# Norm stage: the shared down product in one tile shape and two banks, the low part in two instructions; table stage: constants in another order

## Time and profile before

| | us |
|---|---|
| median of the timed runs (3) | 3653.11 (3651.51 to 3653.34) |
| the profiled execution, time | 3649.46 |
| its span | 3647.7 |
| norm stage, from to | 0 to 414 |
| table stage | 414 to 453 |
| attention with the experts | 453 to about 3433 |
| output | to the end |
| granted PE clock, mean | 0.984 of full |

### The profile page before, as it was taken

How to read it: one execution, slowest core, us unless ns; L and a number is a source line. 1 busy time by engine, 2 the same in 40 slices (tenths; PEclk the granted TensorE clock), 3 DMA queues, 4 the chain that set the end, 5 groups by cost and what they waited for, 6 DMA issues and landing times. The chain is left out here.

```text
span 3647.7 us, 59807 instructions
## 1 busy us (share of the span) xinstructions
PE 3527.4 (97%) x16231; PEld 2094.8 (57%) x16232; DVE 2534.3 (69%) x3254; ACT 1686.6 (46%) x3126; POOL 2711.4 (74%) x2322
## 2 busy tenths in 40 slices
PE   7999569999999999999999999999999999999899
PEld 5777445555555555555555555555555555555487
DVE  7888657777777777777777777777777777777444
ACT  4444324444444444444444444444444444444443
POOL 1111138888888888888888888888888888889611
PEclk9999779999999999999999999999999999999899
DMA  7766455666666666666666666666666666664386
GB/s 217 218 200 208 155 125 125 160 171 171 171 171 171 171 171 171 171 171 171 171 171 171 171 171 171 171 171 171 171 171 171 171 171 171 171 171 125 118 313 228
DMA packets 393627, 635.53 MB, mean 174 GB/s; under 512 B 48048, under 2 KB 214640, under 8 KB 393584
## 3 DMA queue, kind: packets, MB, share of 16 engines
q1 hardware_dynamic: 370800, 603.54, 59.4%
q0 software_dynamic: 14336, 23.08, 3.0%
q10 hardware_dynamic: 8448, 8.39, 0.6%
HBM read 306.91 MB, written 126.12 MB: 119 GB/s over the span
## 5 line engine op out<-in xcount | busy, mean ns | idle before, releaser
L1089 DVE TENSOR_REDUCE merged<-psum 128x1 f32<-128x1024 f32 x1024 | 1206.2, 1220 | 731.0 <-PE psum L917 729.2
L1052 ACT ACTIVATE probs<-psum 128x512 f32<-128x512 f32 x2048 | 1083.6, 600 | 1159.5 <-PE psum L891 744.4
L1216 POOL TENSOR_TENSOR sums<-sums,probs 128x512 f32<-128x512 f32 x768 | 981.0, 1277 | 94.9 <-ACT probs L1052 40.2
L1217 POOL TENSOR_TENSOR sums<-sums,probs 128x512 f32<-128x512 f32 x768 | 982.4, 1279 | 0.0
L932 PE MATMUL psum<-probs,v_sb 128*64 128x512 f32 x4096 | 930.2, 596 | 0.0
L888 PE MATMUL psum<-q_full,k_full 128*128 128x512 f32 x2048 | 877.3, 428 | 0.0
L891 PE MATMUL psum<-q_rest,k_rest 65*128 65x512 f32 x2048 | 812.5, 397 | 0.0
L932 PEld LDWEIGHTS psum<-probs,v_sb 128*64 128x64 f32 x4096 | 283.7, 137 | 559.2 <-issue 496.1
L888 PEld LDWEIGHTS psum<-q_full,k_full 128*128 128x128 f32 x2048 | 388.5, 190 | 196.6 <-issue 95.3
L1117 DVE RECIPROCAL sum_all<-sum_all 128x128 f32<-128x128 f32 x512 | 448.8, 918 | 28.3 <-ACT sum_all L1060 28.3
L964 PE MATMUL psum<-x_t,w_qk 128*128 128x512 f32 x1536 | 411.9, 404 | 38.0 <-DVE w_d L1082 27.5
(11 more groups left out here) (143 smaller groups left out, 3085.2 us busy)
## 6 DMA issues: line engine op xcount, KB each, us to landing
x_t<-xt SPq DMA_DIRECT2D x118, 1024.0 KB
k_full<-high SPq DMA_DIRECT2D x256, 256.0 KB
v<-values SPq DMA_DIRECT2D x64, 512.0 KB, 3.2
w_qk<-wqk_parts SPq DMA_DIRECT2D x64, 512.0 KB, 4.0
q_full<-high SPq DMA_DIRECT2D x128, 256.0 KB
q_full<-low SPq DMA_DIRECT2D x128, 256.0 KB
k_rest<-low SPq DMA_DIRECT2D x128, 256.0 KB
q_rest<-high SPq DMA_DIRECT2D x128, 256.0 KB
```

Of the source, the lines that this page charges most:

```text
L1052: nc.scalar.activation(probs[:, kt, h, :], ring[ring_place(g, j) % RING], ACT.Exp, scale=SCALE).then_inc(probs_ready, 1)
L1089: nc.vector.tensor_reduce(out=merged[:, col:col + 1], in_=work[:, 2 * h:2 * h + 2, :].rearrange("p b c -> p (b c)"), axis=AX, op=ALU.max, ...
L1216: nc.gpsimd.tensor_tensor(sums[:, half, 0, :], first[:, 0, :], probs[:, kt, 0, :], ALU.add)
L1217: nc.gpsimd.tensor_tensor(sums[:, half, 1, :], first[:, 1, :], probs[:, kt, 1, :], ALU.add).then_inc(sums_added, 1)
```

## The change

- The second tiles of the down product's operands, `ws_d1` and `hidden1`, get 128 partitions; partitions 64 to 127 are set to zero once, by DVE at the start, and PE waits for that (`rest_zero`) in the first unit. All down matmuls then use 128 rows.
- The second round of the down product goes to bank 4 (`up_ps`) and doesn't wait for a copy. In the next unit, the c = 1 products wait for the first copy, the up products for the second.
- POOL's low part is two instructions of 512 columns.
- Table stage: the triangle `upto` is finished first, then the iotas, `carry` last. PE's counting matmuls wait for `ones` alone, its rows for `upto`.

```
-    ws_d1 = sb("ws_d1", [F2, D])
+    ws_d1 = sb("ws_d1", [P, D])
...
-    hidden1 = sb("hidden1", [F2, HALF])
+    hidden1 = sb("hidden1", [P, HALF])
...
-        sp.dma_start(ws_d1[:], io["ws_d"][P:F, :]).then_inc(weights_in, DMA)
+        sp.dma_start(ws_d1[0:F2, :], io["ws_d"][P:F, :]).then_inc(weights_in, DMA)
...
-            nc.gpsimd.tensor_tensor(xt_low[:, par], xt32[:, par], f32(xt_high[:, par]), ALU.subtract
-                                    ).then_inc(xt_lows, 1)
+            for k in range(KD):
+                last = nc.gpsimd.tensor_tensor(xt_low[:, par, k, :], xt32[:, par, k, :], f32(xt_high[:, par, k, :]),
+                                               ALU.subtract)
+            last.then_inc(xt_lows, 1)
...
                 act.wait_ge(down_filled, 2 * u + n + 1)
+                bank = up_ps if n else down_ps
                 nc.scalar.copy(shared[:, par, 2 * n:2 * n + 2, :],
-                               down_ps.rearrange("p (t d) -> p t d", d=D)).then_inc(shared_ready, 1)
+                               bank.rearrange("p (t d) -> p t d", d=D)).then_inc(shared_ready, 1)
...
+        nc.vector.memset(hidden1[F2:P, :], 0.0).then_inc(rest_zero, 1)
+        nc.vector.memset(ws_d1[F2:P, :], 0.0).then_inc(rest_zero, 1)
         norm(0, 0, linked(0, [0]))
...
-                pe.wait_ge(*((shared_ready, 2 * u) if c else (hidden_ready, 2 * (u - 1) + 1)))
+                pe.wait_ge(*((shared_ready, 2 * u - 1) if c else (hidden_ready, 2 * (u - 1) + 1)))
             for out, col in ((down_ps, 2 * P),) if c else ((gate_ps, 0), (up_ps, P)):
+                if out is up_ps and not known(u, 1):
+                    pe.wait_ge(shared_ready, 2 * u)
...
             pe.wait_ge(hidden_ready, 2 * u + 2)
+            if known(u, 1):
+                pe.wait_ge(rest_zero, 2)
             for n in range(2):
-                if n or not (isinstance(u, int) and u == 0):
-                    pe.wait_ge(shared_ready, 2 * u + n)
+                bank = up_ps if n else down_ps
                 for t in range(2):
                     cols = slice((2 * n + t) * P, (2 * n + t + 1) * P)
-                    nc.tensor.matmul(down_ps[:, t * D:(t + 1) * D], hidden0[:, cols], ws_d0[:],
+                    nc.tensor.matmul(bank[:, t * D:(t + 1) * D], hidden0[:, cols], ws_d0[:],
                                      start=True, stop=False)
-                    last = nc.tensor.matmul(down_ps[:, t * D:(t + 1) * D], hidden1[:, cols], ws_d1[:],
+                    last = nc.tensor.matmul(bank[:, t * D:(t + 1) * D], hidden1[:, cols], ws_d1[:],
                                             start=False, stop=True)
...
         nc.gpsimd.memset(ones[:], 1.0).then_inc(consts, 1)
         nc.gpsimd.memset(upto[:], 1.0).then_inc(consts, 1)
-        nc.gpsimd.memset(carry[:], 1.0).then_inc(consts, 1)
+        pool.wait_ge(consts, 2)
+        nc.gpsimd.affine_select(out=upto[:], in_=upto[:], compare_op=ALU.is_ge, fill=0.0, base=0,
+                                pattern=[[1, P]], channel_multiplier=-1).then_inc(consts, 1)
...
-        pool.wait_ge(consts, 6)
-        nc.gpsimd.affine_select(out=upto[:], in_=upto[:], compare_op=ALU.is_ge, fill=0.0, base=0,
-                                pattern=[[1, P]], channel_multiplier=-1).then_inc(consts, 1)
+        nc.gpsimd.memset(carry[:], 1.0).then_inc(consts, 1)
+        pool.wait_ge(consts, 7)
         nc.gpsimd.memset(carry[:, :, 0:1], 0.0).then_inc(consts, 1)
...
-        pe.wait_ge(consts, 8)
+        pe.wait_ge(consts, 1)
         flat = masks[:].rearrange("p j e -> p (j e)")
...
+        pe.wait_ge(consts, 3)
         for n in range(8):
             pe.wait_ge(counts_out, n + 1)
```

More of the change, by code:

```diff
@@ L157, in norm_stage @@
     pads_stored = sem("pads_stored")
+    rest_zero = sem("rest_zero")
     x_v = io["x"].rearrange("(u t p) d -> u p t d", p=P, t=UNIT)
@@ L457, in unit @@
                     dve.wait_ge(down_filled, 2 * u)
-                nc.vector.tensor_tensor(hidden[:], up_rest[:] if c else up_ps, silu[0:rows, c, :], ALU.mult
+                nc.vector.tensor_tensor(hidden[0:rows, :], up_rest[:] if c else up_ps, silu[0:rows, c, :], ALU.mult
                                         ).then_inc(hidden_ready, 1)
             assert count[0] == VEC or not more, count[0]
+        nc.vector.memset(hidden1[F2:P, :], 0.0).then_inc(rest_zero, 1)
+        nc.vector.memset(ws_d1[F2:P, :], 0.0).then_inc(rest_zero, 1)
         norm(0, 0, linked(0, [0]))
```

## The result

| | before | after |
|---|---|---|
| median of the timed runs | 3653.23 (4 runs, 3651.51 to 3653.65) | 3610.26 (4 runs, 3606.79 to 3610.97) |
| the profiled execution, time | 3649.46 | 3610.97 |
| its span | 3647.7 | 3609.2 |
| attention's first matmul starts | 454.45 | 408.39 |
| from there to the end of the span | 3193.25 | 3200.81 |

The ratio is 0.9881, with a 95% interval of 0.9864 to 0.9898: 43 us faster. The forecast was 3610.

What follows compares the result with a forecast made beforehand. PE was taken to bound the norm stage, with DVE close behind. Gains 8.8 + 26.6 + 1.0 + 2.0 + 4.4 = 42.8, say 43 us, off the median 3653.11 gave 3610 us, range 3600 to 3626.

Steps and rivals of the forecast that it cites:

- first three units (third S): Start of the norm stage: third unit's S at 89.5 instead of 98.30, gain 8.8 us (bounds 7.8 and 10.2).
- S: Start of the first down product of a unit in the norm stage, the mark for periods.
- twelve periods: Norm stage, third to fifteenth unit's S: period 21.52 instead of 23.74 us, gain 26.6 us.
- last unit: End of the norm stage: DVE now decides, 19.72 instead of 20.76 us, gain 1.0 us.
- S to the last copy, to the table stage: After the last S of the norm stage: 3.9 us instead of 5.93, gain 2.0 us.
- table stage: PE's counting waits for the ones alone, not all eight constants: gain 4.4 us (bounds 4.1 and 4.6).
- two-unit loop: Norm stage: PE's router product, DVE's chain, PE to the router product after the next: 43.03 us per two units.
- The down product: Norm stage: one shape, two banks, 0.228 us per record; S to second gate/up group 5.02 instead of 7.31 us.
- rival B: Down product: pitch stays 0.63 us even in one shape, only the bank wait goes; 3630 us, chance 0.07.
- rival C: Norm stage: POOL and DVE still meet; 3627 us whole, 3617 with the halves; chance 0.15.
- The new wait: Norm stage: up matmuls wait for the previous unit's second copy; half a microsecond covers it, price zero.
- rival D: Norm stage: PE falls to half clock in each unit after longer idle before S; 3684 us, chance 0.02.

Runs made afterwards that it cites:

- e2: Kernel before with the padding alone: all down products on 128 rows, one bank, its copy still waited for; 3631.86 us, ratio 0.9931.
- e3: Kernel before with the second bank alone, second-tile products still on 64 rows; 3632.95 us, ratio 0.9940.
- e4: Changed kernel with POOL's low part in one whole instruction again; 3609.18 us, ratio 0.9878.
- e8: Kernel before with unread matmuls added in the table stage (84) and the attention's head (5 and 7 at a time); 3646.60 us, ratio 0.9979.
- e9: Kernel before with 128 partitions set aside for the second tiles but only 64 used, no memset; 3653.34 us, ratio 0.9998.
- e10: Changed kernel without the padding: two banks, halved low part, new constants' order, second-tile products on 64 rows; 3634.12 us, ratio 0.9946.
- e1: Kernel before with only POOL's low part in two instructions and the table stage's new constants' order; 3650.08 us, ratio 0.9991.
- e7: Changed kernel run once more, untouched, on the same chip as e5 and e6; 3607.30 us, ratio 0.9883.
- e6: Changed kernel with e5's matmuls plus 5 unread after each projection and 7 after each value group in the attention's head; 3600.53 us, ratio 0.9862.
- e5: Changed kernel with 84 unread matmuls on TensorE in the table stage, before the attention; 3608.58 us, ratio 0.9884.

## Why the prediction was right, and where its terms were not

The terms against the profile of after, by the same marks:

| term | forecast | measured |
|---|---|---|
| first three units (third S) | 8.8 | 98.36 - 87.64 = 10.7 |
| twelve periods | 26.6 | 26.4 |
| last unit | 1.0 | 2.4 |
| S to the last copy, to the table stage | 2.0 | 2.2 |
| table stage | 4.4 | 4.4 |
| sum | 42.8 | 46.1 |
| the head of the attention | 0 | -4.2 |
| its steady part and the output | 0 | -3.3 |
| the profiled pair | 42.8 | 38.5 |

**Bottleneck.** Right: PE set the stage, with DVE close behind, and with the change both are in the loop. The two-unit loop was forecast at 43.03 and is 43.07 (12 periods from 87.64 to 346.06, 21.535 each).

**The down product.** Right in mechanism, 0.1 us too dear: the pitch is 0.216 per record, not the 0.228 that the fp32r records gave, and S to the second group is 4.94, not 5.02. That gained nothing in the period, since DVE takes over; it shows in the 2.2 of the stretch behind the last S. The lower bound of 0.22, set because no row of the norm stage showed less, lies above what came. The attention stage of the kernel before had the row: the experts' down product is two 256-column fp32 products on 128 rows, at full clock, 0.43 us from one to the next, 0.216 per record.

```profile
3150.53 0.59 PE L989 MATMUL psum<-w_d,hidden_e 128*128 128x256 f32 x2
3150.96 0.59 PE L990 MATMUL psum<-w_d,hidden_e 128*128 128x256 f32 x2
```

So "for 256-column fp32 no row of this case shows it" is wrong: these rows could have put rival B out before any run.

**The rule.** Rival B is out by e2: the products of one shape, two rounds of four, keep 0.43, with every load under the matmul before. The Trainium skill (TensorE: Matmul & The Clock Gate, The mechanism) ties the overlap of a load to another row group; the trace disagrees, 0.43 in one row group against 0.63 where the rows change. The sentence of the same page (Part 2, Step-by-step) on a background buffer for weights is the one that these rows bear out. Another page, TensorEngine Tiling (Array Packing), Key Properties, says that a change of the tiling mode drains TensorE; the 0.2 us per change in e3 agree with that, and the page gives no price. Not each change of the number of rows pays it. In the attention stage of the kernel before, fp32r products on 128 and on 65 rows take turns at 0.23 to 0.24 us, no more than such products of one shape (0.23):

```profile
3350.59 0.40 PE L891 MATMUL psum<-q_rest,k_rest 65*128 65x512 f32 x1
3350.83 0.40 PE L888 MATMUL psum<-q_full,k_full 128*128 128x512 f32 x1
```

**POOL and DVE.** Right: they no longer meet, and rival C is out. The forecast left 0.3 between them; 0.17 and 0.64 by turns came. The part of the edit that was made for this is not what did it (e4).

**The new wait.** Right at zero, with 0.59 of cover (0.5 forecast), counted to the up matmuls; their weight load starts at 199.97, 0.37 after the copy.

**First three units.** The step that was mis-sized is S of the third at 89.5: it is 87.64. 0.7 came one unit earlier, 0.45 of it as follows: the chain of the second unit was taken to start "at 43.13 as before", but ACT's cast of the weights came at 38.52 instead of 38.99, DVE's split lost its wait of 0.35, and the chain began at 42.68. The rest is the clock. It fell, as forecast, after a gap of 1.78 (2.3 forecast), but for about 3.5 us instead of the six or more that the sum took: S to the gate was 5.06 in that unit, 1.7 above 3.37, where 3.5 was priced. And PE had 0.48 of wait left before the third S: DVE's chain (65.89 to 87.58) decided it, and hid what the half clock cost. The 10.7 itself is no firm number: the same norm stage as before's put the third S at 99.00 in e8 and 100.23 in e9.

**The half clock's trigger.** The text under rival D says of such a fall: "It decides from a gap of about 1.8", and upward. That rule is wrong. A gap of 0.86 was followed by a fall in e3 and one of 0.74 in e10, gaps of 2.20 and 2.21 (e4) and 3.00 (e2) by none:

```profile
88.48 0.70 PE L546 MATMUL psum<-ws_d,hidden 128*128 128x256 f32 x2 [2.21 <-DVE hidden L460]
```

Windows of four us from 60 to 104 show e4 and e2 at 1.00 around these gaps. So the length of the one gap before it doesn't decide whether the clock falls; what does wasn't found. Rival D didn't come: from the fourth unit on the clock stays at 1.00.

**Last unit.** The step that failed is "DVE takes 402.83 - 383.16 = 19.67, plus 0.05: it now decides". That 19.67 was read off a trace in which DVE waited 3.74 us for ACT's exponential, and so for PE's gate:

```profile
393.35 3.35 DVE L454 RECIPROCAL silu<-exp_g 128x512 f32<-128x512 f32 x1 [3.74 <-ACT exp_g L336]
```

In the trace of after it still waits 1.54 us there, at 353.85. With PE earlier the wait shrank with it: DVE's chain ran from 346.13 to 363.34, 17.2 us, and PE's own 18.56 (forecast 18.5) decided. An interval between two marks isn't an engine's work as long as there is a wait in it.

**Table stage.** Right to the tenth, alone too (e1: 4.4).

**Later stages.** "The later stages don't change and keep their length" is not what the pair showed. The clock in the attention's head comes in patterns: the ten profiled executions without added matmuls in it have heads of 103.5 to 109.2 us, 104.8 and 108.9 with the same kernel (e7). The steady part was 3.3 longer, for a reason that stays open (e9). The profiled execution of before was a short one in this as well, and shifting by 3.65 to the median of before made up for half of the 7.6 given back, by no mechanism that the prediction named. The medians gained 43.0 and (e7) 3651.55 - 3607.30 = 44.3, the work before the attention 46.1. The difference of 2 to 3 is smaller than the intervals (6 us each way), so no more is said of it than that the clock in the head is large enough to make it.

## What to carry to other kernels

Matmuls in a stream that alternate between 64 and 128 rows paid 0.2 us at each change; zeros up to the full rows cost nothing on TensorE and took it away. Look for such a row in every stage of the trace before forecasting: here the experts' down product already had the price of the padded form. A chain of an engine must be cut at its waits before it is set against another engine's: here one wait inside 19.67 us turned the order of two engines around. When a stage ahead is shortened, look how sparse the next one is: its clock may take back some us, and filling its idle stretches with matmuls that nobody reads was worth 6 to 7 us (e6, e8).

## What was not expected of the hardware

- A VectorE instruction that reads two operands from SBUF was held by the GpSimd instruction under way and ended 0.54 to 0.55 us after it, wherever the two met in the norm stage: 2.27 us behind one of 2.38, 1.16 behind the first of two halves (e1), 1.6 where it began 0.2 us into the second (e10), 0.73 to 0.89 where only its tail was left (e2 from the fifth unit on), 0.68 alone. The hold goes both ways: in e1 the second half, under way together with the product, took 1.72 us instead of 1.29. The trace agrees with the Trainium skill (GPSIMD Engine Reference, 1. Specifications) that the two share SBUF interfaces when a VectorE instruction has two SBUF inputs.
- The granted clock fell after 0.74 us of idle (e10) and not after 2.21 (e4) at the same place of nearly the same code, before the third S; nor after 3.00 one unit earlier (e2).
- 84 matmuls right before the attention kept the clock up for its first projection only (1.91 us against 2.93) and were worth nothing in the median (e5); 5 or 7 between each two steps of the head kept it up through most of it (e6: 0.83 in the first 10 us, 0.97 to 1.00 in the next 50).
- A 256-column fp32 product, two records, took 0.43 us at full clock in a stream and 0.85 at half (66.23 to 67.08 in the second unit of after).
